# A spectral convolution with 145 blocked 128x128 solves: deeper staging buffers, a new split of the work formed ahead, and the copies of solved blocks moved from GpSimd to ScalarE

## The reference

```
x -> x + conv_ref(group_norm(x), weight, bias)          x: (32, 128, 32, 32)
conv_ref:
  xfft = rfft2(pad(x, 1))                      34 x 18 frequencies, used as 34*18 systems
  V    = rfft2(weight, s=(34, 34))             128 x 127 per frequency
  G    = V^H V + eps * I,  eps = 1e-5 * mean(diag)
  W    = I - 2 V solve(G, V^H)
  z    = irfft2(W @ xfft)[crop] + bias
```

## Time and profile before

| what | us |
|---|---|
| median of 3 runs | 3236.74 (3235.59 to 3256.79) |
| the profiled execution | 3247.75 |
| its span, first to last instruction | 3246.0 |
| mean granted TensorE clock | 0.857 of 2.4 GHz |

### The profile page before, as it was taken

How to read it: one execution, slowest core, us unless ns; L and a number is a source line. 1 busy time by engine, 2 the same in 40 slices (tenths; PEclk the granted TensorE clock), 3 DMA queues, 4 the chain that set the end, 5 groups by cost and what they waited for, 6 DMA issues and landing times. The chain is left out here.

```text
span 3246.0 us, 89212 instructions
## 1 busy us (share of the span) xinstructions
PE 2670.2 (82%) x38313; PEld 2156.6 (66%) x38313; DVE 2019.4 (62%) x3842; ACT 1280.1 (39%) x2979; POOL 733.6 (23%) x1307
## 2 busy tenths in 40 slices
PE   5985655899889989989876869677888888859999
PEld 3375653555646577877865757466677677759999
DVE  5056440478797877967959888797887781002333
ACT  1331321434424345555543535343455544532222
POOL 0600000212121022422422313041343233420000
PEclk7587787989899999999988989797998899976787
DMA  4525245223131135745625335160231133455673
GB/s 177 103 67 113 57 57 106 79 96 110 48 133 51 51 63 114 139 85 113 138 51 106 63 70 112 21 131 10 92 102 50 54 104 97 130 134 138 169 185 99
DMA packets 562600, 310.02 MB, mean 96 GB/s; under 512 B 484616, under 2 KB 495496, under 8 KB 561368
## 3 DMA queue, kind: packets, MB, share of 16 engines
q1 hardware_dynamic: 520896, 183.58, 27.6%
q0 software_dynamic: 41312, 120.73, 11.2%
HBM read 162.85 MB, written 141.30 MB: 94 GB/s over the span
## 5 line engine op out<-in xcount | busy, mean ns | idle before, releaser
L1350 DVE SCALAR_TENSOR_TENSOR arena<-arena,psum 128x512 f32<-128x512 f32 (+2 forms) x608 | 399.0, 719 | 292.6 <-PE psum L981 292.2
L1313 DVE TENSOR_TENSOR arena<-arena 128x960 f32<-128x960 f32 (+24 forms) x480 | 419.0, 873 | 16.6
L1308 DVE TENSOR_TENSOR arena<-arena 128x960 f32<-128x960 f32 (+8 forms) x600 | 406.4, 727 | 8.2
L918 PE MATMUL psum<-arena 128*32 128x256 f32 (+1 forms) x2904 | 267.9, 433 | 115.7 <-DMA arena<-plain 74.5
L835 POOL COPY arena<-arena 128x512 f32<-128x512 f32 (+2 forms) x160 | 86.8, 588 | 1149.3 <-ACT arena L1123 1149.3
L960 PEld LDWEIGHTS psum<-arena 32*32 32x32 f32 x9280 | 156.8, 116 | 246.0 <-issue 231.7
L981 PE MATMUL psum<-arena 32*128 32x64 f32 x9280 | 311.4, 282 | 9.8 <-ACT arena L1144 9.8
L981 PEld LDWEIGHTS psum<-arena 32*128 32x128 f32 x9280 | 290.2, 196 | 34.0 <-ACT arena L1144 20.4
L960 PE MATMUL psum<-arena 32*32 32x64 f32 x9280 | 182.7, 232 | 126.3 <-DVEq L1342 114.7
L922 PE MATMUL psum<-arena 128*32 128x256 f32 (+1 forms) x3696 | 267.8, 374 | 0.0
L1123 ACT COPY arena<-arena 32x128 f32<-32x128 f32 (+3 forms) x496 | 222.0, 448 | 31.3 <-DVE arena L1350 12.5
(11 more groups left out here) (121 smaller groups left out, 4867.5 us busy)
## 6 DMA issues: line engine op xcount, KB each, us to landing
blocks<-arena POOLq DMA_DIRECT2D x145, 256.0 KB, 2.5
arena<-blocks SPq DMA_DIRECT2D x290, 128.0 KB, 2.8
kept<-arena POOLq DMA_DIRECT2D x145, 256.0 KB, 3.1
arena<-kept SPq DMA_DIRECT2D x145, 256.0 KB, 2.9
xhat<-arena SPq DMA_DIRECT2D x32, 580.0 KB, 13.0
arena<-xhat SPq DMA_DIRECT2D x580, 32.0 KB, 2.6
yhat<-arena POOLq DMA_DIRECT2D x290, 64.0 KB, 2.5
arena<-x SPq DMA_DIRECT2D x8, 2048.0 KB, 10.3
```

Source lines behind the costliest of these rows:

```text
L918: pe.matmul(columns[quadrant(p)].rearrange("p (a k) n -> p a k n", k=m), K["ident"][:, quadrant(p)], spread(base[:, 0:m, :], 1, n), start= ...
L1308: ins = dve.tensor_tensor(pr, spread(R[:, t, :, :, j], 3, 2 * w_), both, ALU.mult)
L1313: link(dve.tensor_tensor(rest, rest, pr[:, :, h], op))
L1350: ins = dve.scalar_tensor_tensor(old, old, K["mask"][:, piv:piv + 1], upd_bank(u, c)[:, 0:L * n].rearrange("p (t n) -> p t n", n=L), ALU.m ...
```

## The change

Four things change.

1. `PRE` becomes 45, 45, 45, 10 in place of 42, 42, 42, 19.
2. `staged` has 8 buffers in place of 2, each with its own semaphore: `copy_blocks` waits for the store of 8 quads earlier, not of 2.
3. The tail's loads go to 8 new buffers (`tail_in`) in place of the 4 of `part_in`. They lie over the first 16 quads' place in `M`, which is free once `final a` is done. A buffer is loaded again when the quad 8 places earlier is summed. Final a keeps its four.
4. `copy_p` and `copy_q` are ScalarE's. GpSimd keeps the stores and `reset`. ScalarE now waits for the last update of `M` (`upd_copied`) at the head of each `mid` and `final` job.

```diff
-PRE = [0, 42, 84, 126, NQ]
+PRE = [0, 45, 90, 135, NQ]
+NST, NTAIL = 8, 8
-        staged = early(2, QUAD, 2 * L)
+        staged = early(NST, QUAD, 2 * L)
+        tail_in = Carve(BASE_SOLVE)(NTAIL, QUAD, 2 * L)
+        TAIL = before("final", len(jobs) - 1)
+        def part_of(m):
+            n, buf = (m, part_in) if m < TAIL else (m - TAIL, tail_in)
+            slots = 4 if m < TAIL else NTAIL
+            return buf[:, n % slots], S[f"{'part' if m < TAIL else 'tail'}_in{n % slots}"], 16 * (n // slots + 1)
...
                     def load_part(m):
-                        if m >= 4:
+                        if m >= TAIL:
+                            sp.wait_ge(S["y_done"], max(TAIL, m + 1 - NTAIL))
+                        elif m >= 4:
                             sp.wait_ge(S["y_done"], m - 3)
...
@@ GpSimd, job "mid" @@
-                            pool.wait_ge(S["upd_copied"], 2 * before("sweep", at))
                             for m in range(lo, hi):
-                                copy_p(m)
-                                if m > lo:
-                                    store_part(m - 1)
-                            store_part(hi - 1)
+                                store_part(m)
...
@@ GpSimd, job "final" @@
-                            for m in range(lo, min(lo + 4, hi)):
-                                copy_q(m)
                             for m in range(lo, hi):
                                 store_y(m)
-                                if m + 4 < hi:
-                                    copy_q(m + 4)
...
@@ ScalarE @@
+                    def copy_p(m):
+                        if m >= 2:
+                            act.wait_ge(S["s_done"], m - 1)
+                        src = M[:, home(mid_quads[m]), :, :]
+                        dst = emb[:, m % 2, 1].rearrange("p f q r m -> p (f q) r m")[:, :, 0, :]
+                        act.copy(dst, src.rearrange("p f n -> p (f n)").rearrange("p (a b) -> p a b", b=B))
+                        act.copy(work[:, m % 2, :, 0:L], src).then_inc(S["p_copied"], 1)
...
-                            act.wait_ge(S["upd_done"], before("sweep", at))
+                            act.wait_ge(S["upd_copied"], 2 * before("sweep", at))
                             copy_b(lo)
+                            copy_p(lo)
                             copy_j(lo)
                             for m in range(lo, hi):
                                 copy_t(m)
                                 if m + 1 < hi:
                                     copy_j(m + 1)
+                                    copy_p(m + 1)
                                 copy_s(m)
...
+                            act.wait_ge(S["upd_copied"], 2 * before("sweep", at))
                             for m in pairs[0]:
                                 copy_jq(m)
+                                copy_q(m)
...
                                 for m in pairs[n + 1] if n + 1 < len(pairs) else ():
                                     copy_jq(m)
+                                    copy_q(m)
```

More of the change, by code:

```diff
@@ L800, in load_part @@
                         q = final_quads[m]
-                        if m >= 4:
+                        if m >= TAIL:
+                            sp.wait_ge(S["y_done"], max(TAIL, m + 1 - NTAIL))
+                        elif m >= 4:
                             sp.wait_ge(S["y_done"], m - 3)
+                        part, landed, _ = part_of(m)
                         sp.wait_ge(S[f"part_stored{q % 2}"], 16 * (mid_quads.index(q) // 2 + 1))
-                        sp.dma_start(part_in[:, m % 4, :, :].rearrange("p f n -> p (f n)"), kept[q]).then_inc(
-                            S[f"part_in{m % 4}"], 16)
+                        sp.dma_start(part.rearrange("p f n -> p (f n)"), kept[q]).then_inc(landed, 16)
                     for at, (kind, g, k, lo, hi) in enumerate(jobs):
@@ L837, in reset @@
                         ins.then_inc(S["reset"], 1)
[L839 to L852, removed]
                     def store_blocks(m):
                         pool.wait_ge(S["pre_copied"], m + 1)
-                        pool.dma_start(blocks[m].rearrange("p (f n) -> p f n", f=QUAD), staged[:, m % 2]).then_inc(
-                            S[f"pre_stored{m % 2}"], 16)
+                        pool.dma_start(blocks[m].rearrange("p (f n) -> p f n", f=QUAD), staged[:, m % NST]).then_inc(
+                            S[f"pre_stored{m % NST}"], 16)
                     def store_part(m):
@@ L1034, in turn_q @@
                     def turn_q(m):
-                        pe.wait_ge(S[f"part_in{m % 4}"], 16 * (m // 4 + 1))
+                        part, landed, count = part_of(m)
+                        pe.wait_ge(landed, count)
                         pe.matmul(psum[m % 2][:, 0:256], K["nturn"],
@@ L1038, in turn_q @@
                         pe.matmul(psum[m % 2][:, 256:256 + QUAD * NB].rearrange("p (f n) -> p f n", f=QUAD), K["turn"],
-                                  part_in[:, m % 4, :, NB:2 * NB], start=True, stop=True).then_inc(S["q_turned"], 1)
+                                  part[:, :, NB:2 * NB], start=True, stop=True).then_inc(S["q_turned"], 1)
                     def solve_z(m):
@@ L1212, in _ @@
                             if before("pre", at):
-                                for n in range(2):
-                                    act.wait_ge(S[f"pre_stored{n}"], 16 * len(range(n, NQ, 2)))
+                                for n in range(NST):
+                                    act.wait_ge(S[f"pre_stored{n}"], 16 * len(range(n, NQ, NST)))
                             for u in range(lo, hi):
```

30 lines of the change are left out of this document (16 added, 14 removed).

## The result

The changed kernel takes 3153.43 us (median of 4 runs, 3133.91 to 3154.81); the kernel before takes 3239.4 beside it (median of 4). The two medians are 86 us apart; the ratio of all runs is 0.971, interval 0.966 to 0.976, which is 94 us less. The forecast was 62 us less, 3175 us. Sign and order are right; by the ratio a third of the gain was missing from the sum. Run again on another chip, the changed kernel took 3150.68, a ratio of 0.9746 (0.9704 to 0.9787).

The account below looks back on a forecast made before the run. No engine was full, so limits were read stage by stage: DVE beside mid b, PE and ACT in mid a. Gains of 27 + 0 + 6 + 23 + 6 = 62 us from 3236.7 gave 3175 us, range 3147 to 3207.

Parts of the forecast that it names:

- Part A: Mid b: without GpSimd's copies DVE's factor gets shorter, 6.7 us a stage counted, 27 us less over four stages.
- rival 2: Sweeps behind pre and mid b: the lower clock takes part E and a part of A, 3201 us; chance 0.16.
- Part B: Mid a: ScalarE's two new copies, 0.83 us, fit in a 1.25 us gap of the loop; cost 0.
- Part C: Final a: DVE gains 3.3 us a stage, PE leaves room for it in three stages; 6 us less.
- Part D: Tail: eight buffers end PE's wait for kept, a pair takes 5.10 us, the tail 170; 23 us less.
- rival 4: Tail: another wait, for the stores of ys, replaces the load's; gain 6 us, not 23; 3192 us; chance 0.12.
- Part E: Pre: third and fourth sweeps start 20 us earlier in sum, 14 go back to the clock; 6 us net gain.
- Rivals 1, 3 and 4: 1: ScalarE becomes the bound, 3305, chance 0.04; 3: GpSimd's stores, not copies, hold DVE, 3208, 0.07; 4: as rival 4.

Follow-up runs that it names:

- part 4 alone: The kernel before with only copy_p and copy_q moved to ScalarE, old buffers and old split: 3183.87 us against 3229.55, ratio 0.985.
- part 3 alone: The kernel before with only the tail's eight load buffers, copies on GpSimd: 3188.51 us, ratio 0.987.
- parts 1 and 2: The kernel before with eight staging buffers and the split 45, 45, 45, 10, old tail, copies on GpSimd: 3221.5 us over 10 runs, ratio 0.997.
- parts 1 to 3: The changed kernel with the copies back on GpSimd: 3189.83 us, ratio 0.984 to the kernel before.
- both splits: The changed kernel with PRE split 44, 44, 44, 13 and with 44, 43, 43, 15: 3135.65 and 3141.62 us, ratios 0.970 and 0.972.
- six buffers: The changed kernel with 6 load buffers in the tail in place of 8: 3137.13 us, ratio 0.968.
- the deep buffers: The changed kernel with the tail's eight buffers serving from the second part of final a on: 3140.74 us, ratio 0.969.
- part 2 alone: The kernel before with only eight staging buffers, split 42, 42, 42, 19, copies on GpSimd: 3230.8 us over 10 runs, ratio 1.0016.

## Why the prediction was right or wrong, point by point

In short, the waits that the prediction named were the right ones, and the sum was 32 us short. The largest miss is the tail, whose pair was priced at 5.10 us and takes 4.75 (14 us). The others are a term put at nothing, PE's wait for GpSimd's copies at the heads of the jobs (8 us in mid a, and a part of final a's 9), and the 14 us that the sweeps behind pre were to give back to the clock, of which they gave back 7. Mid b gave 5 less.

The profiles of the runs put each stage on more than one execution, without and with the part of the change that bears on it:

| stage | without the part | with it | difference | forecast |
|---|---|---|---|---|
| pre (parts 1, 2) | 566.3, 543.7, 548.5, 552.0; mean 552.6 | 539.2, 539.3, 539.4, 538.2; mean 539.0 | -14 | -6 |
| mid a (part 4) | 506.7 to 512.7, mean 510.1 | 496.9 to 506.2, mean 502.4 | -8 | 0 |
| mid b (part 4) | 562.2 to 584.5, mean 569.3 | 532.4 to 557.4, mean 547.7 | -22 | -27 |
| final a (part 4) | 432.0 to 455.7, mean 440.8 | 414.1 to 431.7, mean 425.8 | -15 | -6 |
| tail (part 3) | 188.6 to 199.1, mean 192.5 | 155.6, 155.7, 155.7, 156.4; mean 155.8 | -37 | -23 |

For pre the left column holds the kernel before twice, part 4 alone and part 3 alone, the right one the changed kernel twice, parts 1 and 2, and parts 1 to 3. For the tail the left column holds five executions with four buffers, the right one the changed kernel twice, part 3 alone and parts 1 to 3. For part 4 the left column holds six executions (before twice, parts 2, 1 and 2, 3, and 1 to 3), the right one six or seven (the changed kernel twice, part 4 alone, both splits, six buffers, and in mid a and mid b the deep buffers). Before rounding the differences add up to -95; the ratio gave -94. The runs of the parts say the same without any profile: part 4 alone 47 us by its ratio, part 3 alone 41, parts 1 and 2 10, together 98, each with 11 to 18 us either way.

**Part A was right in its mechanism.** DVE's factor beside mid b fell by 7.1 us of busy time a stage; part 4 alone shows it, and its absence in the run of parts 1 to 3 shows it again. The Trainium skill's page SBUF — State Buffer (section "SBUF: two separate sides") describes an exclusive lock on the port pair that GpSimd shares with VectorE. The measured 94.17 against 87.03 agrees with a lock that the copies take, and so do single instructions that take 942 ns in place of 199. The stores cost DVE nothing visible: in the changed kernel's fourth pre stretch, with 10 of them, it is busy for 86.56 us, in the three others, with 45 each, for 86.65 to 86.72. The term was 27, and up to the start of the sweeps just that came: on average PE's fillers and waits in mid b take 335.8 us in place of 363.0. The stage gave 22 because the four sweeps took 211.9 us in place of 206.3. The first of them took 48.5 to 49.0 in the six executions without part 4 and 48.6 with part 4 alone, but in six of seven with part 4 and the new buffers 52.5 to 56.1, at a granted clock of 0.80 to 0.86. That is rival 2 in a small size. What sets it stays open.

**Part B was right for the loop** (3.60 before and after), and failed at the head of the jobs, in the step "GpSimd was no faster there. I take 0": GpSimd was slower. Mid a lost 8 us, of which 5.5 are in its fillers. PE's waits ahead of `solve_b` in mid a, before and then after (L1000 is the old L1014):

```profile
PE psum L1014 <- issue: 9.3, 7, 2.7
PE psum L1014 <- POOL arena L845: 5.7, 1, 5.7
...
PE psum L1000 <- ACT arena L1163: 8.0, 4, 5.1
```

The rows named "issue" are waits for GpSimd too: each of these seven ends 0.10 us after an L845, as the one for POOL does 0.15 after. At a head GpSimd first makes `reset`'s copies. In the second job PE's `turn` starts at 1303.41, GpSimd's `reset` ends at 1307.27, its L845 at 1307.96, and `solve_b` starts at 1308.06, 4.65 us after `turn`. In the changed kernel `solve_b` starts 2.88 us after `turn` (1277.22 - 1274.34), since ScalarE has made both copies by 1276.70 and `copy_j` by 1277.17. Over mid a these waits come to 15.1 to 17.5 us in the six executions without part 4 and 7.1 to 8.3 in the seven with it, 8 us less on average, of which the rest of the fillers takes some 3 back. In mid b they fall from 14.2 to 19.6 down to 4.2 to 4.5, and there DVE hides it.

**Part C failed in its size.** The step was "3.3 a stage" and "nothing in the fourth": DVE gained 4.2 a stage, 0.20 us a copy. I had PE's fillers fixed as well. They are 5 us shorter in sum, PE's waits ahead of the sweeps are 6 shorter, and the sweeps 4; the forecast had only the second. Of the fillers' 5 us, 4 are again the heads of the jobs, where PE waited for GpSimd's `copy_q`:

```profile
PE psum L1045 <- POOL arena L852: 4.2, 3, 1.4
```

It is 4.2 to 5.4 us in the six executions without part 4 and at most 0.6 with it. The sweeps' 4 us are the clock: two of the six executions on the left, those of part 2 alone and of parts 1 to 3, took 451.2 and 455.7 us, with sweeps as low as 0.70. Without these two the stage gives 9 and not 15.

**Part D failed in the step "where a pair ran without a DMA wait"**. The pair of the earlier trace rows did have one. The PE row shows no idle time, since the matmul before it is drawn until its modelled end, 2738.81, and the next starts at 2738.94. The weight loads of the same stretch show it:

```profile
2736.81 1.86 PEld L1045 LDWEIGHTS psum<-arena 128*128 128x128 f32 x16 [0.20 <-issue]
2738.94 0.30 PEld L1036 LDWEIGHTS psum<-arena 128*128 128x128 f32 x2 [0.27 <-DMA arena<-kept]
```

From L1045 to L1036 it is 2.13 us there and 1.83 in the changed kernel's pair (2701.12 - 2699.29). That is 0.30 of the 0.35 us, and the rest is in the matmul behind the wait. Without it a pair is 4.75, and 31.5 pairs are 149.6 us in place of 160.7. That is 11 of the 14 us. The other 3 are in the 7 us set aside for drops of the clock, of which 3.4 were used: the first pair took 7.59 us at a granted clock of 0.61, and one took 5.85 at the full clock. Part 3 alone shows it all, and with it that rival 4 was wrong: its sign came, `copy_y` waited for `yhat` 12 times, 10.2 us in the changed kernel, but PE did not.

**Part E failed in the step "I put the third sweep at 53"**, and in taking the first two sweeps' 58.6 and 57.1 for what a wait for DVE costs. Starts 9 and 11 us earlier were right, and so was the fourth sweep (55.4 and 55.3 in the changed kernel's two executions). But with eight buffers the waits of 5.3, 3.1 and 5.9 us were followed by 49.2, 50.0 and 49.8, and so were waits of 8 to 11 us in the run of part 2 alone. The third sweep took 49.8 to 50.0, not 53. Against the one profile the stage gave 27 us; against four executions of the old code it gave 14: about 20 from the earlier starts, as forecast, less about 7 that the sweeps gave back, where the forecast had 14. More than half of the surprise was the profile itself.

The Trainium skill's rule (TensorE: Matmul & The Clock Gate, section "Why this matters for your kernels") agrees with the fourth sweep, 55.4 at 0.80 behind a wait of 7.4 us against 45.5 at 1.00 behind 0.5. For the first three it would have had the price wrong, as I had. Why the fourth is hit and the others not stays open. In six executions with the new split it took 55.3 to 55.5 us behind waits of 7.4 to 8.0, but in the run of parts 1 to 3 it took 47.8 behind a wait of 7.7.

One thing about part E does not close. Staging alone shortens its stage by 15 us against the mean of 552.6, but ten runs show no gain (1.0016). Their granted clock was 0.852 to 0.858, that of the runs of before up to 0.867. In the one profile of it the time comes back in final a, 451.2 us against 432.0 and 435.5 in the kernel before, and in the tail, 199.1 against 193.4 and 191.0, both at a lower granted clock. Why it is lower there, and whether the other nine runs are like it, stays open.

Rivals 1, 3 and 4 fell, each by a run of its own. Rival 2 was half right: it took 6 us from A, and in part E the forecast had already taken too much for it.

## What to carry to other kernels

Read the shortest clean period of a loop from the engine's weight loads as well as its matmuls before multiplying it by 31: a wait of 0.3 us hid under a modelled end here, and that was 11 us. The shortest of 31 spacings may still hold a wait. Where a row says "issue", look at what other engines finish just before it ends: here it was a copy queued on GpSimd behind others, 8 us that no term had. A copy taken from GpSimd pays where VectorE is the bound and ScalarE has a gap of known length, which the loop's timeline shows. And before a price is read from how two like stretches differ in clock, take a second execution: here half of a 27 us difference was in the profile and not in the kernel.

## What the hardware showed that I had not expected

- Two copies of 128x256 on GpSimd for each quad cost VectorE 0.22 us per copy in its own instructions. The price falls on single instructions, one of which took 942 ns in place of at most 199. Stores issued from GpSimd cost VectorE nothing that can be seen (86.56 us a factor beside 10 of them, 86.65 to 86.72 beside 45).
- The tail without gaps had the higher granted clock: 0.97 to 0.99 in the nine executions with six or eight buffers (in the changed kernel PE was busy 99% of the time), 0.93 to 0.96 in the five with four, with the same instructions of PE.
- A sweep of group a took 45.5, 47.3, 50, 55.5 or 58.6 us in different places and executions, with the granted clock between 1.00 and 0.77. The whole program varies with it: 17 runs of before on one chip lay between 3206 and 3252 us, with mean granted clocks between 0.857 and 0.867, the lower ones mostly in the slower runs.
